# Fewer tiles of scattered and gathered rows in flight in the routed tail

## The reference

```python
x = x + _L1_ffn_ref(_layernorm(x, axis=-1), router_w, expert_weights)

# _L1_ffn_ref
logits = jnp.einsum('bsh,eh->bse', x, router_w)
rw = jax.nn.softmax(logits, axis=-1).reshape(T, E)
vals, idx = jax.lax.top_k(rw, TOP_K)                  # TOP_K = 2, E = 32
w_masked = jnp.zeros_like(rw).at[jnp.arange(T)[:, None], idx].set(vals)
# over all experts e:
acc + x_flat * w_e[:, None] @ W_e
```

## Time and profile before

| | us |
|---|---|
| median of 3 timed runs | 3046.83 |
| their lowest and highest | 3045.23, 3049.2 |
| the profiled execution | 3051.39 |
| its span | 3049.6 |
| PE busy | 2463.2 (81%) |
| ACT busy | 1796.3 (59%) |
| DVE busy | 1570.5 (51%) |
| POOL busy | 734.8 (24%) |

### The profile page before, as it was taken

One profiled execution on the slowest core, in us unless ns is written; L12 is line 12 of the kernel. 1 busy time (PEld: TensorE's weight loads), 2 busy tenths in 40 slices (PEclk: granted clock), 3 DMA queues, 4 the chain that ended last, 5 costly groups with the idle time before them and its releaser, 6 DMA issues. The chain is left out here.

```text
span 3049.6 us, 63240 instructions
## 1 busy us (share of the span) xinstructions
PE 2463.2 (81%) x24662; PEld 1422.4 (47%) x24666; DVE 1570.5 (51%) x2607; ACT 1796.3 (59%) x2682; POOL 734.8 (24%) x1006
## 2 busy tenths in 40 slices
PE   6888888875888898589999999999998662659643
PEld 4555555544676565334333333333334551547432
DVE  5768676687764676454554455444542670210212
ACT  3534435353554454379999999999995230426221
POOL 3202030300000367312211122212210317340434
PEclk9999999987899899789999999999998776779866
DMA  7800000002000144656667656766652433556546
GB/s 253 269 1 2 1 1 1 1 1 44 1 1 1 40 154 152 127 97 105 128 118 122 109 97 132 119 118 105 109 87 72 129 122 116 176 169 210 183 149 232
DMA packets 251996, 308.83 MB, mean 101 GB/s; under 512 B 100544, under 2 KB 180160, under 8 KB 251584
## 3 DMA queue, kind: packets, MB, share of 16 engines
q1 hardware_dynamic: 237344, 269.49, 37.4%
q0 software_dynamic: 12288, 33.57, 3.3%
q10 hardware_dynamic: 2080, 1.84, 0.2%
HBM read 157.23 MB, written 147.59 MB: 100 GB/s over the span
## 5 line engine op out<-in xcount | busy, mean ns | idle before, releaser
L1790 ACT ACTIVATE at_PT<-at_pS 128x1024 f32<-128x1024 f32 (+2 forms) x1152 | 1002.5, 1224 | 14.5 <-PE at_pS L1817 14.5
L1648 POOL TENSOR_SCALAR_AFFINE_SELECT at_PT<-at_PT 128x256 f32<-128x256 f32 (+1 forms) x384 | 196.3, 520 | 827.1 <-ACT at_PT L1790 826.8
L1817 PE MATMUL at_pS<-hd_QT,hd_KT 99*32 99x512 bf16 (+3 forms) x5120 | 319.0, 351 | 6.3 <-DVE at_QT L1762 4.9
L1817 PE MATMUL at_pS<-at_QT,at_KT 99*32 99x512 bf16 (+3 forms) x5120 | 315.4, 348 | 4.1 <-issue 1.6
L2361 PE MATMUL tl_bank<-tl_W,tl_xT 128*128 x896 | 242.8, 413 | 72.8 <-issue 65.1
L1835 PE MATMUL at_pO<-at_PT,at_V 128*32 128x512 f32 (+3 forms) x2560 | 289.3, 529 | 4.5 <-issue 4.3
L1835 PE MATMUL at_pO<-at_PT,hd_V 128*32 128x512 f32 (+3 forms) x2560 | 290.4, 529 | 2.8 <-issue 2.8
L1738 DVE COPY at_OT<-at_pO 128x512 f32<-128x512 f32 x64 | 44.3, 691 | 481.1 <-PE at_pO L1835 476.8
L1817 PEld LDWEIGHTS at_pS<-hd_QT,hd_KT 99*32 99x32 bf16 x5120 | 113.6, 95 | 262.4 <-ACT at_PT L1790 167.9
L1817 PEld LDWEIGHTS at_pS<-at_QT,at_KT 99*32 99x32 bf16 x5120 | 113.8, 95 | 258.5 <-ACT at_PT L1790 165.5
L451 ACT ACTIVATE la_ft<-la_ft 128x1024 f32<-128x1024 f32 x128 | 135.2, 1056 | 161.4 <-DVE la_ft L274 161.3
(11 more groups left out here) (352 smaller groups left out, 4252.5 us busy)
## 6 DMA issues: line engine op xcount, KB each, us to landing
tl_xin<-rows_in SPq DMA_DIRECT2D x56, 512.0 KB
rows_out<-tl_yout SPq DMA_DIRECT2D x56, 512.0 KB
score_terms<-at_parts SPq DMA_DIRECT2D x60, 384.0 KB, 5.8
rows_in<-la_zeros SPq DMA_DIRECT2D x8, 2048.0 KB, 7.6
rotated_qk<-qk_qkT SPq DMA_DIRECT2D x16, 1024.0 KB, 4.3
at_qk<-rotated_qk SPq DMA_DIRECT2D x60, 256.0 KB, 4.2
rows_in<-la_zeros SPq DMA_DIRECT2D x4, 3072.0 KB, 11.2
values<-qk_rv SPq DMA_DIRECT2D x64, 192.0 KB, 4.6
```

The costliest lines, as they stand in the source:

```text
L1648: nc.gpsimd.affine_select(out=d, in_=d, compare_op=ALU.is_ge, fill=0.0, base=0, pattern=of, channel_multiplier=-1).then_inc(masked, 1)
L1790: nc.scalar.activation(PT[u % 6][:, 0:banks, 0:width], pS[u % 3][:, 0:banks, 0:width], ACT.Exp, scale=HD ** -0.5).then_inc(exp_done, 1)
L1817: last = mm(pS[u % 3][r:r + 32, b, col:col + 512 - off], KT[par][0:KS, h, kb * P + r:kb * P + r + 32], QT[par][0:KS, h, c * 512 + off:(c + ...
```

## The change

`NS_`, the number of slots for gathered tiles, goes from 4 to 2, and `NO`, the number of semaphores (and so of tiles) for scattered tiles in flight, from 8 to 2. The slots' addresses, the waits and `wait_sent` follow from these two numbers; the order of all instructions stays as it is. The buffer `ay` keeps its size.

```diff
-    NB, NX, NY, NS_, NO = 4, 4, 2, 4, 8
+    NB, NX, NY, NS_, NO = 4, 4, 2, 2, 2
```

## The result

The change makes the kernel **faster by 3.7%**: 2932.9 us (median of 4 runs, 2927.2 to 2936.2) against 3046.0 for the kernel before, measured beside it; the ratio is 0.963, with a 95% interval of 0.961 to 0.964. The forecast was 3066.3 us, slower, with a range of 3049 to 3083. Both the sign and the range were wrong. The profiled execution of after took 2927.2 us, with a span of 2925.4.

A forecast was written before the change was run, and what follows sets the result against it. The prediction took the first five indirect-DMA bursts, with PE held back, and the sixth at the kernel's end as the bound. Scatters +1, gathers +9 and last burst +9.5 made +19.5 us, so 3066.3 us, range 3049 to 3083.

The forecast's parts named there:

- What bounds the kernel: Tail: the first five indirect-DMA bursts lie on the path nearly whole, PE held back; the sixth ends the kernel.
- Part 1: Scatter bursts, two tiles in flight instead of eight: no stall on quiet queues, +1 us, bounds 0 and +4.
- Part 2: Gather bursts 4 and 5, two tiles in flight instead of four: +9 us, bounds 0 and +20.
- steady price: Gathers after a burst's opening: a pair of tiles takes 5.38 us instead of 5.01, +0.37 us a pair.
- the openings free: Openings of bursts 4 and 5: each grows by 5 us, unpaid because PE works on through it.
- Part 3: Last gather burst, at the kernel's end: 51 us against 41.3, +9.5 us, bounds 5 and 13.
- the gather beside the output's stores: Last burst: a tile's second gather takes 6.2 us while stores fill the queues, a pair 8.8 us, until about 3022.
- (c): Bursts 4 and 5: PE's slow phase needs a POOL pace above some limit; slower pace frees PE, 2996 us; chance 0.08.
- (b): Bursts 1 to 5: PE gets back what POOL leaves idle, so they cost nothing; +9.5, 3056 us; chance 0.25.
- (a): All bursts: all growth is paid, openings too, as PE's slow phase follows burst length; +33.5, 3080 us; chance 0.17.
- (d): Next to nothing: VectorE's adds catch up in the last burst, the steady gap is hidden; 3049 us; chance 0.10.
- The two prices: Skill-page checks: 2.3 us per POOL DMA, so no steady cost; ring turn-taking, so +8 us in the last burst.

The follow-up runs named there:

- quarter-pause kernel: Kernel before plus a POOL memset of 0.33 us after each tile's two indirect DMAs: 3023.5 us, ratio 0.994; in a lower-level set 2844.9 us, 1.005.
- half pause: Kernel before plus a POOL memset of 0.54 us after each tile's two indirect DMAs: 2872.4 us, ratio 0.944; in a lower-level set 2861.1 us, 1.011.

## Why the prediction was wrong, step by step

**What bounds the kernel: right.** The bursts lie on the path because PE is held back in them. "What holds PE back no row names" was left at that and treated as a constant. The runs name it as far as they go: indirect DMAs issued without a gap. How these reach PE stays open.

**Part 1, scatters +1: wrong, measured -53 us.** The forecast confined slow landings to the openings of bursts 1 and 3, "before PE falls silent". That is a row of the kernel before, and the silence was itself what the burst did. In after the opening's slow landings make POOL pause, PE doesn't fall silent, SP's transfers go on, and landings stay slow through the burst: 3.45 and 3.38 us a tile. Burst 2 opens with no such traffic, and there the forecast held: 2.60 us a tile, no stall to speak of, -1.8 us. The quiet latency was 3.14 us instead of 2.8, still under the 3.8 (5.07 - 1.27) at which a stall begins, so that error cost nothing.

**Part 2, gathers +9: wrong, measured -61 us for that edit alone, the last burst's loss included.** Two steps failed. The steady price of 5.38 us a pair was built on 2.81 us of latency, read where PE was silent; with PE working, VectorE starts 4.3 us after a tile's second gather in the mean of burst 5, and up to 6.9, and pairs take 7.1 to 7.6 us (twice 3.57 and 3.78). This made bursts 4 and 5 longer by far more than 9 us: 32 tiles at 3.57 instead of 2.54 are +33. And the growth was taken "in full, since a pause of 0.37 us in 5.38 is short". The pauses were 1.7 us in the mean and up to 4.3, and with them PE ran through the bursts: the interval from burst 5 to 6 fell by 36 us. The step that had the openings free because PE "kept its speed for the first 5 to 11 DMAs" was read as a count of DMAs. It was a pace: 32 and more DMAs pass at the slower pace and PE runs on.

**Part 3, the last burst +9.5: right in sign, twice too large.** It measured 44.6 us from first to last gather against 40.0, so +4.6, just under the lower bound of 5; to the end of the span +5.0. The term that was mis-sized is the gather beside the output's stores, 6.2 us until 3022, for 2.3 pairs. That collision isn't there any more. The source view of the stores gives their first and last start:

```profile
L1984 SPq DMA_DIRECT2D out_dram<-all_X x16: 372/1123/1582, 2840.6 to 2922.1; - x16
```

Before they began at 2998.99, 3 us ahead of the burst; after, PE and SP are done earlier against the gathers and they begin 32 us ahead of it, at 2840.6, in burst 5. The DMA share of burst 6 falls from 0.79 to 0.45. What is left is the steady price, which was about right: many pairs stand 5.4 to 5.5 us apart, with two pauses such as these in each.

```profile
2886.74 0.95 POOL L2018 DMA_INDIRECT tl_ay<-rows_out,all_dest  x1 [0.54 <-DVE all_X L2217]
2889.46 0.95 POOL L2018 DMA_INDIRECT tl_ay<-rows_out,all_dest  x1 [0.53 <-DVE all_X L2217]
```

One pair of 7.7 us among them brings the mean to 5.76, where before it was 5.16 (twice 2.58). The forecast's own addition was slightly off as well: its terms give 20 + 30.7 + 0.5 - 41.3 = 9.9, not 9.5, which decides nothing.

**The rivals.** What came true is (c), which had 0.08: PE's slow phase needs a pace above a limit. Its argument was right in kind, and three of its parts were wrong. It placed the limit between 1.25 and 1.345 us a DMA; measured it lies between 1.36 and 1.47 (half of 2.72 and 2.93), and if the mean pace is what counts, the forecast's new pace of 1.345 would not have been slow enough. The 1.44 us that the text held against it lies inside that bracket. It left PE half its rate, where in bursts 4 and 5 PE did nearly all of its work. And it took only bursts 4 and 5. Hence 2996 instead of 2933. (b), PE gets back what POOL leaves idle, had the right direction but treated it as an even exchange, microsecond for microsecond; 128 pauses of 0.33 us gave back 21 us, 128 of 0.54 us 170 us. (a) and (d) have nothing for them.

**The two prices.** For the first the Trainium skill, "DMA: Bandwidth & Descriptors", section on the SWDGE path, gives 2.3 us for these bytes (estimate from the page); the quiet scatter measured 3.14 us including POOL's answer of 0.28, so 2.9. The difference decided nothing. The turn-taking between rings that the Trainium skill states on the same page, section on queues, made the last burst +8 rather than +9.5 in the prediction (by its own terms 9.1 rather than 9.9); since twelve stores at once no longer stand at that burst's opening, no run here bears on it.

**What should have been seen.** The sum took the landing times of a stretch in which PE was silent, and asked of PE's recovery only whether it had time. The two belong together. Had the question been what a PE that keeps working does to the landings, the answer stood in the earlier trace rows, 5.6 and 6.7 us, and with it pairs of 8.2 and 9.3 us by the prediction's own sum, 3 to 4 us above 5.01 instead of 0.37. Measured were 2.1 to 2.6 above it.

## What to carry to other kernels

Where one engine is silent beside another's burst, don't price a new wait with the latencies of that silence: work out both ends, silent and working, since each may keep itself going. Where many indirect DMAs lie beside PE's work, try a short gap after every two of them, here a memset of 0.54 us on POOL. It gave 5.6 to 5.8% with nothing else changed, more than the smaller number in flight did, but try it in more than one session and put none where no PE work lies beside: in two sets out of five there was nothing to win, and it cost about 1%.

## What the runs showed of the hardware that I had not expected

- **Indirect DMAs issued back to back hold PE back.** At one per 1.27 us PE starts 89 matmuls in 82 us; at two per 2.93 us 393 in 94 us. Between the two the effect goes over in a step of 0.2 us a tile. A busy POOL (93 of 109 us) or as many bytes in plain DMAs (one per 0.54 us, 178 matmuls in 45 us) don't do it. This holds at the higher of the two levels below.
- **The same kernel has two levels**, 3042 to 3046 us and 2827 to 2830, between sets of runs; all runs of one set agree on one. At the lower one the identical quarter-pause kernel isn't held back; the kernel before has no trace there. The change was measured at the higher level only; its gain of 3.7% is the gain there.
- **PE's granted clock is not what holds it back.** In burst 2 of after it is the lower level, 1.2 GHz, but PE is busy for 2.6 of 30 us there, so the low clock goes with the idle time:

```profile
2510.00:2540.00 30.00, 2.63 (x8) 2.21 (x9) 0.00 (x0) 1.19 (x2) 21.25 (x23) 0.50 0.38 131
```

With the half pause the same burst has 0.94 of the full 2.4 GHz.
